# Second half's high parts parked in DRAM, low parts left in place; one gate tile in a third buffer

## Chip, cores and metric

One Trainium2 chip, one of its cores. The metric is the device time of one execution in microseconds, the median of the runs shown. Every time below is in microseconds unless it says ns.

## What is computed

The input `x` holds 32 sequences of 64 rows with 1024 values. A state-space convolution (a kernel of length 1024 for each of the 64 channels, masked by each sequence's length) makes a matrix of 2048 rows (tokens) by 1024. A feed-forward block with 4-bit packed weights follows, and its result is added to `x`:

```
x2    = conv(x).reshape(2048, 1024)
w[k,n] = q[k,n]*s[k//128, n] - (z[k//128, n] + 1)*s[k//128, n]
gate  = x2 @ Wg            # 1024 x 2752
up    = x2 @ Wu            # 1024 x 2752
inter = gate * sigmoid(gate) * up
out   = x + (inter @ Wd).astype(float16)    # Wd: 2752 x 1024
```

## The kernel before, in words

The convolution comes first and leaves its result in SBUF. The second half of the rows (1024 tokens) stays as plain float32 in `y2` until it is needed. The matrix products take their operands in the reduced 32-bit form, so that every moving operand is split into a high part (a cast) and a low part (value minus high part), and each product is made twice, once with each.

The feed-forward block then runs in tiles `tau` = 0 to 43: 22 tiles of 128 intermediate columns for the first 1024 rows, and the same 22 for the second 1024 (`NT` = 22 is the first tile of the second half). The last tile of each half (`TAIL` = 21, and `LAST` = 43) is narrow: 64 gate columns and 64 up columns share one gate tile, so it has no up products, and its down products are half as many.

A tile has eight slots `g`, one for each group of 128 input features. In a slot TensorE does `gate(tau, g)` (four matmuls, L1186), `down` of one 128-column piece of an earlier tile (four matmuls, L1225; it lags by 11 slots) and `up(tau, g)` (four matmuls, L1207). ScalarE rescales the gate and up sums between groups (L631, L650). VectorE takes each down piece into `acc` (`take_down`, L951), unpacks weights (`shift`, L889, then `center`, L913; gate in slots 1 and 2, up in 3 and 4, down in 5 and 6), and multiplies gate by up once a tile (`multiply`, L929). GpSimd splits that product into `mid_h` and `mid_l` (`split_mid`, L517 and L520). The down pieces use two PSUM pairs in turn, so `down` number n waits for `take_down` number n-2.

The order of work on every engine is written out by hand, and so is that of the DMA queue: SyncE issues the weight loads in `LOAD_ORDER` into a ring of four buffers `q_in`, each load waiting until the one four places before it has been centered.

At the border of the halves the operand `xs` is replaced. In tile 21 ScalarE casts `y2` into the high parts of `xs` as soon as the gate products of a group have used the old ones (L660), and GpSimd makes the low parts (`split_x2`, L527), four before `split_mid(21)` and four behind it. `gate(22, g)` waits for them. The narrow tile's down weights are shifted and centered together in slot 7 of tile 21.

At the end, `down_last` (L1243) does the 16 half-width pieces of tile 43, of which GpSimd sums seven (`BY_POOL`, L555, from what ScalarE has scaled, L670) and VectorE nine (L975). The output of 1024 rows is stored in eight pieces of 512 KB: in six of them TensorE adds `x` and the turned result in PSUM (`rows_first`, L1255, `rows_second`, L1266) and ScalarE copies the sum out (L677); in two VectorE adds (L984). Before `down_last` VectorE splits the narrow product (`split_last`, L965).

Of the kernel before, what the change touches and what calls it, by code (L numbers as in the profile page):

```python
# [16 lines left out]
P = 128  # L17
# [3 lines left out]
KT = L // P  # L21
# [20 lines left out]
TURN_AT, TURN_STEP = 181, 8  # L42
TINY = float(2.0 ** -60)
# [85 lines left out]
def load_order():  # L129
    order = [("g", 0), ("u", 0), ("d", 0), ("g", 1), ("u", 1)]  # L130
    for tau in range(1, TILES):
        order += [("g", tau + 1)] * (tau + 1 < TILES)
        order += [("u", up_after(tau))] * (up_after(tau) is not None)
        order += [("d", tau)]
    return order

# [5 lines left out]
BY_POOL = (0, 3, 5, 7, 9, 11, 13)  # L142
THROUGH_PE = (0, 1, 2, 3, 6, 7)
# [15 lines left out]
def build_program(nc, x, itok, log_dt, C, log_A, A_imag, D, gq, gs, gz, uq, us, uz, dq, ds, dz,  # L159
                  ctab, stab, ident_in, out):  # L160
    kpad = nc.dram_tensor("kernel_padded", (H, KPAD), F32, kind="Internal").ap()
    rows_back = nc.dram_tensor("rows_backwards", (2 * TAIL + 1, 16, G, P), I32, kind="Internal").ap()
    zscr = nc.dram_tensor("zeros_plus_one", (3, ROWS, P), BF16, kind="Internal").ap()
    with ExitStack() as ctx:
# [9 lines left out]
        xs = sb("xs", [P, 2, KT, HALF], F32R)  # L174
# [55 lines left out]
        o16 = sb("o16", [P, NH, HALF], F16)  # L230
        x_fin = sb("x_fin", [P, 4, HID])
# [11 lines left out]
        w["d"][1] = sb("wd1", [P, HID], F32R)  # L243

# [30 lines left out]
        x2_cast, x2_split = sem("x2_cast"), sem("x2_split")  # L275
# [10 lines left out]

        def up_ps(tau):

            return pair[3] if tau else pair[1]

        def last_ps(e):

            return (pair[3], pair[0])[e // 2 % 2][:, e % 2, :]

        def last_turn_ps(tt):
            return pair[3][:, tt % 2, :].bitcast(F16)
# [22 lines left out]
        def _(sp):  # L319
# [138 lines left out]
            for tau in range(1, TILES):  # L458
                if tau + 1 < TILES:
# [26 lines left out]
            for tt in range(HALF_G):  # L486
                if tt in THROUGH_PE:
                    sp.wait_ge(sum_copied, 2 * (THROUGH_PE.index(tt) + 1))
# [7 lines left out]
        def _(pool):  # L496
# [7 lines left out]
            for g in range(HALF_G):  # L504
                pool.wait_ge(x1_cast, g + 1)
                here = slice(P * g, P * g + P)
                pool.tensor_tensor(xs[:, 1, :, here], y_nat[:, g % 2], xs[:, 0, :, here].bitcast(F32), ALU.subtract  # L507
# [16 lines left out]
            def split_x2(kt):  # L524

                pool.wait_ge(x2_cast, kt + 1)
                pool.tensor_tensor(xs[:, 1, kt, :], y2[:, kt, :], xs[:, 0, kt, :].bitcast(F32), ALU.subtract  # L527
                                   ).then_inc(x2_split, 1)

            def cast_out(hid):  # L530

                pool.wait_ge(x2_split, KT)
# [830 lines left out]
```

## Time and profile before

| what | value |
|---|---|
| median of 3 runs | 1199.46 (1198.85 to 1199.54) |
| profiled execution: own time | 1200.26 |
| profiled execution: span of its records | 1198.2 |
| mean granted TensorE clock | 0.992 |
| TensorE matmul busy | 97% |
| VectorE, ScalarE, GpSimd busy | 75%, 72%, 18% |

The span runs from the first to the last record of the core. Busy shares are averages over the whole span; a stage can have another limit than the whole.

### The profile page before, as it was taken

The numbers are of one execution on the slowest core, as the hardware profiler recorded it, in microseconds if no ns is written. First come the engines' busy times: TensorE is split into PE (matmuls) and PEld (weight loads), VectorE is DVE, ScalarE is ACT, GpSimd is POOL, SyncE is SP. The second block draws the span as 40 slices with busy tenths as digits, with TensorE's granted clock in tenths as the row PEclk, the third lists the DMA queues.
The fourth block names the chain that finished last, engine by engine and source line by source line (L and its number), as shares of the span: only waits on it lengthen the run. The fifth ranks groups of instructions, "written<-read, shape, count | busy, mean of one in ns | idle before, by whom it ended". The sixth has DMA issues, their size and how long they took to land.

```text
span 1198.2 us, 15016 instructions
## 1 busy us (share of the span) xinstructions
PE 1164.7 (97%) x5570; PEld 953.6 (80%) x5570; DVE 896.6 (75%) x964; ACT 859.7 (72%) x1408; POOL 213.3 (18%) x126
## 2 busy tenths in 40 slices
PE   5899999999999999999999899999999999999997
PEld 4899999788788788788788678888788788788784
DVE  7698755677777777777777888887777777777775
ACT  6433213888788788788788877778788788788774
POOL 0022000211211211211211851211211211211212
PEclk9899999999999999999999999999999999999999
DMA  8587868434444334444444355555434443444413
GB/s 294 171 263 245 274 222 247 129 99 112 106 102 110 106 103 108 106 106 106 106 106 106 79 176 147 170 169 147 106 100 112 106 104 108 106 105 107 150 59 152
DMA packets 64670, 165.54 MB, mean 138 GB/s; under 512 B 11398, under 2 KB 16966, under 8 KB 64598
## 3 DMA queue, kind: packets, MB, share of 16 engines
q1 hardware_dynamic: 64566, 164.56, 47.8%
q8 instruction: 44, 0.72, 0.3%
q14 instruction: 28, 0.23, 0.1%
q0 software_dynamic: 32, 0.03, 0.0%
HBM read 155.74 MB, written 11.64 MB: 140 GB/s over the span
## 4 chain that ended last, share of the span: by engine, by line
PE 86%; DVE 4%; SPq 3%; issue 2%; DMA 2%; ACT 1%; POOL 0%; ACTq 0%; DVEq 0%; POOLq 0%
PE pair L1186 26%; PE pair L1207 26%; PE pair L1225 25%; PE pair L1143 8%; DMA toep<-kernel_padded 1%; DVE acc L951 1%; SPq L333 1%; ACT pair L631 1%; PE pair L1255 1%; DVE q_in L889 1%; DMA kernel_padded<-k_sb 1%; ACT xs L660 1%; POOL o L555 0%; DVE arg L712 0%; DVE y_nat L847 0%
## 5 line engine op out<-in xcount | busy, mean ns | idle before, releaser
L951 DVE SCALAR_TENSOR_TENSOR acc<-pair,s_down,acc 128x1024 f32<-128x1024 f32 x328 | 420.6, 1283 | 209.1 <-PE pair L1225 209.0
L650 ACT ACTIVATE pair<-pair,ratio 128x512 f32<-128x512 f32 x581 | 360.6, 658 | 130.7 <-PE pair L1207 130.7
L631 ACT ACTIVATE pair<-pair,ratio 128x512 f32<-128x512 f32 x616 | 382.6, 666 | 97.1 <-PE pair L1186 96.7
L1186 PE MATMUL pair<-xs,wg 128*128 128x512 f32 x1408 | 388.7, 398 | 0.1
L1207 PE MATMUL pair<-xs,wu 128*128 128x512 f32 x1344 | 368.7, 395 | 1.9 <-DVE sil L929 1.9
L1186 PEld LDWEIGHTS pair<-xs,wg 128*128 128x128 f32 x1408 | 264.8, 189 | 64.6 <-ACT pair L631 4.1
L1207 PEld LDWEIGHTS pair<-xs,wu 128*128 128x128 f32 x1344 | 249.4, 188 | 67.2 <-issue 11.7
L1225 PE MATMUL pair<-mid_h,wd 128*128 128x512 f32 x688 | 268.6, 392 | 5.4 <-DVE acc L951 5.4
L1225 PE MATMUL pair<-mid_l,wd 128*128 128x512 f32 x672 | 265.8, 396 | 0.0
L517 POOL CAST mid_h<-sil 128x1024 fp32r<-128x1024 f32 (+1 forms) x43 | 45.2, 1051 | 843.2 <-DVE sil L929 841.8
L1225 PEld LDWEIGHTS pair<-mid_h,wd 128*128 128x128 f32 x688 | 129.4, 188 | 37.9 <-DVE acc L951 6.9
L1143 PE MATMUL pair<-u_all,toep 128*128 128x256 f32 (+7 forms) x1024 | 151.9, 310 | 5.2 <-DMA toep<-kernel_padded 5.2
L1143 PEld LDWEIGHTS pair<-u_all,toep 128*128 128x128 f32 x1024 | 147.0, 193 | 9.6 <-DMA toep<-kernel_padded 5.7
L1225 PEld LDWEIGHTS pair<-mid_l,wd 128*128 128x128 f32 x672 | 126.2, 188 | 30.4
L520 POOL TENSOR_TENSOR mid_l<-sil,mid_h 128x1024 fp32r<-128x1024 f32 x42 | 101.8, 2424 | 3.4
L889 DVE TENSOR_SCALAR q_in<-q_in,shifts 128x1024 int32<-128x1024 int32 x130 | 101.8, 783 | 0.0
L642 ACT ACTIVATE sil<-pair,ratio 128x512 f32<-128x512 f32 (+1 forms) x88 | 55.8, 693 | 0.7 <-PE pair L1186 0.7
L913 DVE TENSOR_TENSOR wg<-q_in,z_in 128x1024 fp32r<-128x1024 int32 x44 | 56.1, 1276 | 0.1
L913 DVE TENSOR_TENSOR wd<-q_in,z_in 128x1024 fp32r<-128x1024 int32 x44 | 55.4, 1260 | 0.1
L929 DVE SCALAR_TENSOR_TENSOR sil<-pair,ratio,sil 128x1024 f32<-128x1024 f32 x42 | 53.6, 1275 | 1.2 <-PE pair L1207 1.2
L913 DVE TENSOR_TENSOR wu<-q_in,z_in 128x1024 fp32r<-128x1024 int32 x42 | 51.0, 1215 | 0.0
L507 POOL TENSOR_TENSOR xs<-y_nat,xs 128x1024 fp32r<-128x1024 f32 x8 | 20.0, 2503 | 103.4 <-ACT xs L620 103.4
(156 smaller groups left out, 424.2 us busy)
## 6 DMA issues: line engine op xcount, KB each, us to landing
q_in<-rows_backwards SPq DMA_DIRECT2D x86, 512.0 KB, 4.6
z_in<-zeros_plus_one SPq DMA_DIRECT2D x130, 256.0 KB, 4.6
toep<-kernel_padded SPq DMA_DIRECT2D x64, 512.0 KB, 6.7
q_in<-_L_ffn_down_qweight_dram SPq DMA_DIRECT2D x42, 512.0 KB, 4.6
u_all<-in_x_dram SPq DMA_DIRECT2D x16, 512.0 KB, 9.1
x_fin<-in_x_dram SPq DMA_DIRECT2D x12, 512.0 KB, 8.4
out_dram<-x_fin SPq DMA_DIRECT2D x12, 512.0 KB, 5.3
q_in<-in_x_dram SPq DMA_DIRECT2D x4, 512.0 KB, 5.5
```

The costliest lines, as they stand in the source:

```text
L520: pool.tensor_tensor(low, whole, mid_h[0:n, tau % 2].bitcast(F32), ALU.subtract).then_inc(midl_done, 1)
L631: act.activation(gate_ps[:, tb, :], gate_ps[:, tb, :], ACT.Copy, scale=ratio[:, 0, G * t + g:G * t + g + 1]).then_inc(gate_scaled, 1)
L642: act.activation(sil[to:to + n, tb, :], gate_ps[0:n, tb, :], ACT.Silu, scale=ratio[0:n, 0, G * t + G - 1:G * t + G]).then_inc(gate_scaled, 1)
L650: act.activation(up_ps(tau)[:, tb, :], up_ps(tau)[:, tb, :], ACT.Copy, scale=ratio[:, 1, G * t + g:G * t + g + 1]).then_inc(up_scaled, 1)
L889: dve.tensor_scalar(q_in[slot][:], q_in[slot][:], shifts[:, m == "d":1 + (m == "d")], 15, ALU.logical_shift_right, ALU.bitwise_and).then_i ...
L913: dve.tensor_tensor(to, q, z, ALU.subtract).then_inc(centered, 1)
L929: dve.scalar_tensor_tensor(out=sil[:], in0=up_ps(tau)[:], scalar=ratio[:, 1, G * t + G - 1:G * t + G], in1=sil[:], op0=ALU.mult, op1=ALU.m ...
L951: dve.scalar_tensor_tensor(out=acc[:, hid, :], in0=ps, scalar=scale, in1=acc[:, hid, :], op0=ALU.mult, op1=ALU.add).then_inc(down_taken, 1)
L1143: mm = pe.matmul(conv_ps[half_][k][:, base + B * d:base + 256], toep[:, slot, P * (KT - 1 - d):P * (KT - d)], u_all[:, g, 0:KT - d, B * hh ...
L1186: mm = pe.matmul(gate_ps[:, tb, :], w["g"][tau % 2][:, g, :], xs[:, part, g, 512 * tb:512 * tb + 512], start=g == 0 and part == 0, stop=pa ...
L1207: mm = pe.matmul(up_ps(tau)[:, tb, :], w["u"][full_before(tau) % 2][:, g, :], xs[:, part, g, 512 * tb:512 * tb + 512], start=g == 0 and pa ...
L1225: mm = pe.matmul(down_ps[at % 2][:, tb, :], w["d"][tau % 2][:, P * hid:P * hid + P], mid[:, tau % 2, 512 * tb:512 * tb + 512], start=part ...
```

## The change

- The split of the second half moves from tiles 21 and 22 to tiles 4 to 11, all of it on GpSimd (`split_second`): in tile 4+kt, once that tile's down weights are centered, it casts `y2[:, kt]` into `staged` (512 KB) and subtracts that from `y2` in place, which makes `low_2`. SyncE stores `staged` in a DRAM tensor `high_parts`, behind the load of that tile's down weights, and GpSimd waits for the store before it uses `staged` again.
- At the border SyncE loads the eight high parts (512 KB each) into `high`, each after `gate(21, kt)`; ahead of them stand the loads of gate and up 23, behind them those of down 22 and of four pieces of `x`.
- The gate tile 22 is loaded behind up 22 and shifted and centered in slot 4 of tile 20, into a third buffer. The narrow tile's down weights are shifted in slot 5 of tile 21 and centered in slot 0 of tile 22.
- At the end the last two pieces of tile 42 go to the PSUM pairs of up and gate, `down_last` to the down pairs, the split of the narrow product moves to GpSimd, `BY_POOL` becomes (0, 1, 4, 6, 8, 11, 13), four output pieces go through TensorE and four through VectorE, and the stores go in the order 0, 1, 4, 5, 2, 6, 3, 7.
- `low_1` (first half) lies where `o16` and `x_fin` come later.

```diff
@@ load_order
-        order += [("g", tau + 1)] * (tau + 1 < TILES)
+        order += [("g", tau + 1)] * (tau + 1 < TILES and tau != TAIL)
         order += [("u", up_after(tau))] * (up_after(tau) is not None)
+        order += [("g", NT)] * (tau == TAIL - 1)
         order += [("d", tau)]
...
-BY_POOL = (0, 3, 5, 7, 9, 11, 13)
-THROUGH_PE = (0, 1, 2, 3, 6, 7)
+BY_POOL = (0, 1, 4, 6, 8, 11, 13)
@@ sync
+                if tau == TAIL - 1:
+                    load_weights("g", NT)
+                if tau == NT:
+                    sp.wait_ge(high_stored, 16 * KT)
+                    for kt in range(KT):
+                        sp.wait_ge(gate_mm, 2 * (G * TAIL + kt) + 2)
+                        sp.dma_start(high[:, kt, :].bitcast(F32), high_back[kt]).then_inc(high_in[kt], 16)
                 load_weights("d", tau)
-                if tau == NT + 1:
-                    sp.wait_ge(x2_split, KT)
+                if SPLIT_FROM <= tau < SPLIT_FROM + KT:
+                    sp.wait_ge(high_staged, tau - SPLIT_FROM + 1)
+                    sp.dma_start(high_back[tau - SPLIT_FROM], staged[:].bitcast(F32)).then_inc(high_stored, 16)
+                if tau == NT:
                     for tt in range(4):
                         load_x(0, tt)
@@ gpsimd
+            def split_second(kt):
+                if kt:
+                    pool.wait_ge(high_stored, 16 * kt)
+                else:
+                    pool.wait_ge(y_ready, 2 * NG)
+                pool.wait_ge(centered, load_at("d", SPLIT_FROM + kt) + 1)
+                pool.tensor_copy(staged[:], y2[:, kt, :]).then_inc(high_staged, 1)
+                pool.wait_ge(high_staged, kt + 1)
+                pool.tensor_tensor(low_2[:, kt, :], y2[:, kt, :], staged[:].bitcast(F32), ALU.subtract
+                                   ).then_inc(low_ready, 1)
...
             for tau in range(LAST):
-                if tau == TAIL:
-                    for kt in range(4):
-                        split_x2(kt)
+                if SPLIT_FROM <= tau < SPLIT_FROM + KT:
+                    split_second(tau - SPLIT_FROM)
                 split_mid(tau)
                 if tau == TAIL:
-                    for kt in range(4, KT):
-                        split_x2(kt)
@@ scalar
-                    if tau == TAIL:
-                        act.copy(xs[:, 0, g, :], y2[:, g, :]).then_inc(x2_cast, 1)
@@ vector
-                    if g == G - 1 and tau == TAIL:
+                    if g == 5 and tau == TAIL:
                         shift("d", TAIL)
+                    if g == 0 and tau == NT:
                         center("d", TAIL)
...
                         if g == 4:
                             center("u", up_after(tau))
+                            if tau == TAIL - 1:
+                                shift("g", NT)
+                                center("g", NT)
@@ tensor
+                if tau == NT and g == 0:
+                    pe.wait_ge(low_ready, KT)
                 if tau == NT:
-                    pe.wait_ge(x2_split, g + 1)
+                    pe.wait_ge(high_in[g], 16)
...
+                if tau == LAST - 1 and hid == NH - 1:
+                    pe.wait_ge(last_mid, 2)
+                elif at >= 2 and not (tau == LAST - 1 and hid == NH - 2):
                     pe.wait_ge(down_taken, at - 1)
...
-            down(LAST - 1, NH - 3)
-            down(LAST - 1, NH - 2)
+            for hid in range(NH - 3, NH):
+                down(LAST - 1, hid)
             for e in range(4):
                 down_last(e)
-            down(LAST - 1, NH - 1)
             rows_first(0)
             down_last(4)
             down_last(5)
             rows_first(1)
-            for e in range(6, 12):
+            for e in range(6, 11):
                 down_last(e)
             rows_second(0)
-            down_last(12)
-            down_last(13)
             rows_second(1)
-            down_last(14)
-            down_last(15)
+            for e in range(11, 16):
+                down_last(e)
             rows_first(2)
+            turn_last(4)
+            turn_last(5)
             rows_second(2)
             rows_first(3)
+            turn_last(6)
             rows_second(3)
-            turn_last(4)
-            turn_last(5)
-            rows_first(6)
-            rows_second(6)
-            rows_first(7)
-            rows_second(7)
+            turn_last(7)
```

## Rows read from the trace of the kernel before

**Rows 1.** The page: busy time, share of the span, instructions, by engine.

```profile
PE 1164.7 (97%) x5570; PEld 953.6 (80%) x5570; DVE 896.6 (75%) x964; ACT 859.7 (72%) x1408; POOL 213.3 (18%) x126
```

**Rows 2.** TensorE's timeline at the border: start, duration, operation, count, idle before.

```profile
658.98 1.10 PE L1186 MATMUL pair<-xs,wg 128*128 128x512 f32 x4
...
676.23 1.20 PE L1186 MATMUL pair<-xs,wg 128*128 128x512 f32 x4
...
685.34 0.50 PE L1225 MATMUL pair<-mid_h,wd 128*128 128x512 f32 x1 [3.26 <-DVE acc L951]
...
703.48 1.55 PE L1207 MATMUL pair<-xs,wu 128*128 128x512 f32 x4 [1.93 <-DVE sil L929]
...
710.68 1.10 PE L1186 MATMUL pair<-xs,wg 128*128 128x512 f32 x4
```

**Rows 3.** Busy time by stretch: last columns are granted clock, DMA share, GB/s.

```profile
705.00:707.40 2.40, 2.40 (x8) 1.83 (x7) 0.00 (x0) 1.95 (x3) 2.40 (x2) 0.50 1.08 413
```

**Rows 4.** VectorE's timeline at the border.

```profile
680.87 3.21 DVE L913 TENSOR_TENSOR wd<-q_in,z_in 128x1024 fp32r<-128x1024 int32 x1
684.01 2.46 DVE L951 SCALAR_TENSOR_TENSOR acc<-pair,s_down,acc 128x1024 f32<-128x1024 f32 x2
```

**Rows 5.** GpSimd's timeline at the border.

```profile
680.30 11.20 POOL L527 TENSOR_TENSOR xs<-y,xs 128x1024 fp32r<-128x1024 f32 x4
```

**Rows 6.** Line 660, ScalarE's casts: ns min, median, max; first and last start.

```profile
L660 ACT CAST xs<-y x8: 1047/1088/1137, 660.8 to 675.8; 128x1024 fp32r<-128x1024 f32 x8
```

**Rows 7.** GpSimd's timeline in tiles 5 and 6.

```profile
302.40 1.04 POOL L517 CAST mid_h<-sil 128x1024 fp32r<-128x1024 f32 x1 [18.88 <-DVE sil L929]
...
324.80 1.04 POOL L517 CAST mid_h<-sil 128x1024 fp32r<-128x1024 f32 x1 [18.88 <-DVE sil L929]
325.92 2.40 POOL L520 TENSOR_TENSOR mid_l<-sil,mid_h 128x1024 fp32r<-128x1024 f32 x1
```

**Rows 8.** VectorE's timeline in tiles 5 and 6.

```profile
329.14 0.74 DVE L889 TENSOR_SCALAR q_in<-q_in,shifts 128x1024 int32<-128x1024 int32 x1
330.73 1.28 DVE L951 SCALAR_TENSOR_TENSOR acc<-pair,s_down,acc 128x1024 f32<-128x1024 f32 x1 [0.84 <-PE pair L1225]
```

**Rows 9.** TensorE's timeline in tile 6.

```profile
335.17 0.39 PE L1225 MATMUL pair<-mid_h,wd 128*128 128x512 f32 x1
```

**Rows 10.** The DMA queue's timeline between tiles 5 and 6.

```profile
321.92 0.53 SPq L417 DMA_DIRECT2D q_in<-rows_backwards  x1
```

**Rows 11.** The page's DMA issues: count, size, median from issue to landing.

```profile
z_in<-zeros_plus_one SPq DMA_DIRECT2D x130, 256.0 KB, 4.6
```

**Rows 12.** Line 447, loads of `x`, from 698 to 703.

```profile
DMA to landing us min/median/max: 6.6/7.8/10.1
```

**Rows 13.** TensorE's timeline at the end.

```profile
1166.46 1.08 PE L1186 MATMUL pair<-xs,wg 128*128 128x512 f32 x4
...
1172.68 1.21 PE L1243 MATMUL pair<-mid_h,wd 128*128 128x512 f32 x4 [0.71 <-DVE mid_h L965]
...
1181.75 0.61 PE L1266 MATMUL pair<-ident,o 128*128 128x128 f16 x8 [0.88 <-POOL o L555]
...
1191.19 1.94 PE L1255 MATMUL pair<-q_in,ident 128*128 128x512 f32 x4
```

**Rows 14.** ScalarE's timeline at the end.

```profile
1193.61 1.07 ACT L677 COPY q_in<-pair 128x512 f32<-128x512 f32 x2 [1.15 <-PE pair L1266]
```

**Rows 15.** GpSimd's timeline at the end.

```profile
1180.33 5.08 POOL L555 TENSOR_TENSOR o<-z_in,acc 128x512 f16<-128x512 f32 x4 [0.91 <-ACT z_in L670]
```

**Rows 16.** VectorE's timeline at the end.

```profile
1169.43 2.48 DVE L951 SCALAR_TENSOR_TENSOR acc<-pair,s_down,acc 128x1024 f32<-128x1024 f32 x2
```

**Rows 17.** Line 451, stores from 1160 on: their issues, then issue to landing.

```profile
L451 SPq DMA_DIRECT2D out_dram<-q_in x4: 538/538/586, 1190.0 to 1194.7; - x4
...
DMA to landing us min/median/max: 3.0/3.0/3.7
```

**Rows 18.** Busy time by stretch, as rows 3.

```profile
1192.00:1194.00 2.00, 1.57 (x11) 0.72 (x9) 0.00 (x0) 0.85 (x2) 0.00 (x0) 1.00 1.01 414
```

More of the change, by code:

```diff
@@ L274, in build_program @@
         down_mm, down_taken = sem("down_mm"), sem("down_taken")
-        x2_cast, x2_split = sem("x2_cast"), sem("x2_split")
+        high_staged, high_stored, low_ready = sem("high_staged"), sem("high_stored"), sem("low_ready")
+        high_in = [sem(f"high_in{i}") for i in range(KT)]
         o16_done = sem("o16_done")
@@ L285, in build_program, with parts_of @@
         gate_ps, down_ps = pair[0], [pair[1], pair[2]]
+        def parts_of(tau):
+            return high, (low_2 if tau >= NT else low_1)
         def up_ps(tau):
@@ L458, in _ @@
             for tau in range(1, TILES):
-                if tau + 1 < TILES:
+                if tau + 1 < TILES and tau != TAIL:
                     load_weights("g", tau + 1)
@@ L688, in _ @@
                     copy_sum(1)
-            for tt in THROUGH_PE[2:]:
+            for tt in (2, 3):
                 copy_sum(tt)
@@ L1058, in _ @@
                         continue
-                    if tau + 1 < TILES:
+                    if tau + 1 < TILES and tau != TAIL:
                         if g == 1:
@@ L1087, in _ @@
                     take_last(e)
-            for tt in (4, 5):
+            for tt in range(4, HALF_G):
                 finish_last(tt)
@@ L1184, in gate @@
                         pe.wait_ge(gate_scaled, 2 * (G * tau + g) - 1 + tb)
-                    for part in range(2):
-                        mm = pe.matmul(gate_ps[:, tb, :], w["g"][tau % 2][:, g, :],
-                                       xs[:, part, g, 512 * tb:512 * tb + 512],
+                    for part, rows in enumerate(parts_of(tau)):
+                        mm = pe.matmul(gate_ps[:, tb, :], w["g"][gate_slot(tau)][:, g, :],
+                                       rows[:, g, 512 * tb:512 * tb + 512],
                                        start=g == 0 and part == 0, stop=part == 1, skip_group_check=g > 0)
@@ L1205, in up @@
                         pe.wait_ge(first_up_scaled, g)
-                    for part in range(2):
+                    for part, rows in enumerate(parts_of(tau)):
                         mm = pe.matmul(up_ps(tau)[:, tb, :], w["u"][full_before(tau) % 2][:, g, :],
-                                       xs[:, part, g, 512 * tb:512 * tb + 512],
+                                       rows[:, g, 512 * tb:512 * tb + 512],
                                        start=g == 0 and part == 0, stop=part == 1, skip_group_check=g > 0)
```

92 lines of the change are left out of this document (49 added, 43 removed).

## The prediction

> **What bounds the kernel now.** The page comes first: TensorE is busy for 97% of the span [rows 1], no other engine over 75%. So a saving must take matmul time away (the change takes none) or close the holes in TensorE's own timeline. That timeline is read next. In a steady tile it has none: `split_mid` starts every 22.40 us [rows 7], that is 2.80 a slot, or 0.93 for each of the slot's three blocks of four matmuls. The holes are at the border of the halves and at the end, and the reader is to look at those two stretches only.
>
> At the border, `gate(21, 0)` starts at 658.98 and `gate(23, 3)` at 710.68: 51.70 us [rows 2]. Between them TensorE waits 3.26 us for `take_down` and 1.93 us for `multiply` [rows 2]. VectorE's timeline says why it is late: a `center` that takes 1.22 elsewhere took 3.21 [rows 4] while GpSimd made four low parts without a pause, 680.30 to 691.5 [rows 5]. The takes beside it, which read PSUM, kept their 1.23 each [rows 4]. So the holes come from VectorE's weight unpacking standing behind GpSimd. After the second hole the granted clock was 0.50 (1.2 GHz) in 705.00 to 707.40 [rows 3], and that costs as well.
>
> **Term 1: the border.** I count what TensorE has to do there, with nothing late. Tile 21: eight slots of gate and down, 8 x 1.86 = 14.88, and the `down` ahead of `gate(22, 0)` 0.93: 15.8. The trace took 17.25 (676.23 less 658.98) [rows 2], since ScalarE had a cast of 1.09 in each slot beside its two scalings [rows 6]; the casts are gone. Does the gate bank come free in time? The first half of the last gate product, ScalarE's half of it (about 0.7) and VectorE's (about 0.7) need some 2.1 us after `gate(21, 7)` starts, and TensorE has gate, down, down, 2.8 us, of its own. Yes. Tile 22: slot 0 has no second down (1.86), slots 1 and 2 are full (5.60), from slot 3 on `down` is the narrow one, half of 0.93, so 2.33 a slot: five of them 11.65; then three such slots of tile 23, 7.0. Sum 15.8 + 19.1 + 7.0 = 41.9.
>
> What can be late in it: VectorE. With slot 0 of tile 22 at T, it has two takes to T+2.5, then the `center` of down 21, which stands behind `split_mid(21)` until about T+3.6 and ends at T+4.8. The narrow `down` needs it at T+8.4. From there a shift or center with a take (2.0 and 2.5) goes against slots of 2.33, and `multiply(22)` ends at about T+20.8, where `up(23, 0)` could start at T+20.5. I charge 0.35 for it. So 42.2 against 51.7: **-9.5 us**. Bounds: nothing charged, -9.8; if ScalarE's five operations of about 2.5 a slot and the late take are both felt, some 2 us more, -7.5.
>
> The high parts must be there. Load kt starts after `gate(21, kt)`, the last of them 14 us after the first. Loads of 512 KB packed together landed 6.6 to 10.1 us after issue [rows 12], and each is first read 15 us or more after its issue: hidden. Behind them on the queue stand down 22 (needed at T+14.9) and four pieces of `x`; both have over 5 us. Gate 23 and up 23 are ahead of them, and their buffers are free in tile 20. Tile 20, slot 4 gets a shift and a center more, 0.74 + 1.22. It is hidden by the take's slack: `take_down` of slot 2 ends at 332.0 in tile 6 [rows 8] and the `down` that needs its bank starts at 335.17 [rows 9], 3.2 us later. Without that cover it would cost the 1.96.
>
> **Term 2: tiles 4 to 11.** GpSimd gets a cast and a subtraction, 1.04 + 2.40 by [rows 7], after `center` of the down weights. In the clock of tiles 5 and 6 that center ends at 321.9 (there the queue issues the load that waited for it [rows 10]), so GpSimd is at work to 325.5, and `split_mid`, which started at 324.80, comes 0.8 later and ends at 329.1. Its reader, `down` in slot 3, starts at about 332.4. Hidden.
>
> The wait that is added stands on SyncE. The store waits for `high_staged`, and behind it stands the load of gate tau+2. Before, it was issued at 321.92 [rows 10] for a shift 29.6 us later (329.14 [rows 8] plus a tile). Now it is issued a tile later, at 321.9 + 1.1 (cast) + 0.6 (store's issue) = 323.6, for the shift at 329.14: 5.5 us ahead. A weight load's second part lands 4.6 after its own issue [rows 11], 0.57 later: 328.8 if the store took no bandwidth. At 414 GB/s [rows 18] the store's 512 KB hold the queue 1.27: 330.1. Upper bound of the likely: a load of `x` right behind one weight load landed 6.6 after its issue [rows 12], so 324.2 + 6.6 = 330.8. VectorE's shift is late by 1.0 (bounds 0 and 1.7). Behind it on VectorE stands the take of slot 2, which had 0.84 of idle before it [rows 8] and may itself be late by 3.2 [rows 8, 9] before TensorE stands: 4.0. So **0**, with a margin of 2.3 or more a tile, for eight tiles. Without it each us late would cost eight.
>
> The Trainium skill speaks on the same transfer: "DMA: Bandwidth & Descriptors", section "Anatomy of one DMA", gives a fixed 2.0 us and the bytes at 436 GB/s. As an estimate, store and load (1.31 MB) land 5.0 us after the store's issue, at 328.0, ahead of the shift, where the rows say 330.1; the sum is the same by both.
>
> **Term 3: the end.** All in the clock of before. `gate(43, 7)` starts at 1166.46 [rows 13]; gate and four downs now follow without a hole, to 1171.1. `down_last(0)` needs the take that ends at 1170.7 [rows 16] and GpSimd's split of 64 x 512 (1.27, as its sums [rows 15]), about 1170.9. It starts at 1171.1 instead of 1172.68 [rows 13]. GpSimd has the 4th sum of `BY_POOL` as the one that `rows_second(0)` waits for: piece 6 is multiplied at 1176.9, scaled to 1177.6, summed to 1178.9. So `rows_second(0)` is at 1179.0 instead of 1181.75 [rows 13]. Then copies of 1.07 [rows 14], two fp32 `rows_first` of 1.77, which start at 1182.0 and 1185.3, and adds of about 1.2 give the eight pieces at 1182.0, 1183.7, 1185.7, 1186.9, 1187.5, 1188.8, 1189.4 and 1190.0, the last instead of 1194.7 [rows 17]: 4.7 earlier. But stores are now packed: one alone lands in 3.0, packed ones in 3.7 [rows 17], a step of 1.27 each at 414 GB/s [rows 18] (524 KB). From 1185.7 + 3.0 five more steps give 1195.0, where before it was 1194.7 + 3.0 = 1197.7. So **-2.7 us**. Bounds: unpacked -4.7; if a hand-over in the new order stands 2 us longer, -0.7.
>
> Sum: -9.5 + 0 - 2.7 = -12.2. Profiled span 1198.2 to 1186.0, its own time 1200.26 to 1188.1. The median lies 0.8 below the profiled execution; on it, 1199.46 - 12.2 = **1187.3**.
>
> **The rivals.** (A) Forecast, chance 0.76: own range 1185 to 1190.
>
> (B) The late gate load becomes TensorE's wait in tiles 5 to 12. It decides once the landing is more than 4.0 us behind the shift's place, at 333.1, 8.9 us after the second part's issue. For it: the loads among `x` took up to 10.1 [rows 12], and the store shares the queue. Against it: those had 2 MB ahead, this one has 0.8. At 10.1 the stall is 1.2 a tile, eight tiles 9.6: 1196.9. A milder one, 0.5 a tile, gives 1191.3. Chance 0.10 together, of it 0.03 for the other side: from 1.5 a tile on, twelve and more, the kernel is not faster; at 2 a tile and a half-speed clock behind each hole (some 1 us) it is 24 - 12.2, 1211.
>
> (C) The end gives nothing, as its stores are bound by the DMA engines or the new hand-over waits: -9.5 alone, 1190.0. Chance 0.08.
>
> (D) The border stays half open, because VectorE, not GpSimd, is the limit: the casts' 1.4 us and the first hole go, the second hole and its slow clock (about 3.5) stay: -6 - 2.7, 1190.8. For it: VectorE has 2.0 or 2.5 of work in slots of 2.33. Against it: it was late there by the 3.2 and 2.8 us operations. Chance 0.05. The rest, 0.01, is that the time doesn't change.
>
> One rule would bring (D) or (B) forward. The Trainium skill, "SBUF — State Buffer", section on the two sides of ports: VectorE operations with two SBUF inputs and GpSimd operations lock each other out for a whole instruction, whoever starts first. The trace agrees at the border (3.21 against 1.22). By it a center that starts first could hold GpSimd's split up by 1.2 a tile, still hidden.
>
> **Range and chances.** Eight times in ten: 1185.0 to 1191.5, which takes in (C), (D) and the mild (B). A change of 0.2%, 2.4 us, is what a measurement tells from none. Faster: A, C, D and most of B, 0.95. Same: 0.02. Slower: 0.03.
>
> **What would show it.** Right: no wait over 0.5 between 655 and 700 on TensorE, granted clock 1.00 there, `gate(23, 3)` 42 us after `gate(21, 0)`; tiles 5 to 12 at 22.40, with VectorE's gate shift about 1 us late on a DMA; `rows_second(0)` 2.7 earlier against `gate(43, 7)`; stores of 3.7 and more. Wrong: tiles 5 to 12 over 22.6, with `acc` as TensorE's releaser; a hole before `up(23, 0)` of over 1 us.

## The result and the profile after

The changed kernel takes **1186.56 us** (median, 1184.68 to 1190.44), the kernel before beside it on the same chip 1199.5 (1198.85 to 1201.85). The ratio is 0.9893, with an interval of 0.9863 to 0.9923: 1.1% faster. Predicted were 1187.3.

The profiled execution of after took 1190.44 by its own time, with a span of 1188.7 and a mean granted clock of 0.991. It stands 3.9 above its median, where that of before stood 0.8 above. The reason lies ahead of everything that the change touches: its first tile starts 4.0 later (below). So I read the change from stretches between two marks, not from the two spans.

The page of after, busy time by engine, answers to [rows 1]:

```profile
PE 1158.5 (97%) x5562; PEld 955.3 (80%) x5562; DVE 891.3 (75%) x964; ACT 848.7 (71%) x1396; POOL 220.8 (19%) x136
```

ScalarE has lost its eight casts and GpSimd gained work; TensorE is still the bound. TensorE's timeline of after gives the marks. In order: `gate(21, 0)`, `gate(22, 0)`, the one hole left ahead of `up(23, 0)`, `gate(23, 3)`, `gate(43, 7)`, `down_last(0)`, `rows_second(0)`. It answers to [rows 2, 13].

```profile
662.95 0.39 PE L1224 MATMUL pair<-high,wg 128*128 128x512 f32 x1
...
678.72 0.39 PE L1224 MATMUL pair<-high,wg 128*128 128x512 f32 x1
...
699.48 0.47 PE L1245 MATMUL pair<-high,wu 128*128 128x512 f32 x1 [0.40 <-DVE sil L973]
...
705.08 0.39 PE L1224 MATMUL pair<-high,wg 128*128 128x512 f32 x1
...
1157.93 0.40 PE L1224 MATMUL pair<-high,wg 128*128 128x512 f32 x1
...
1162.51 0.62 PE L1283 MATMUL pair<-mid_h,wd 128*128 128x512 f32 x2
...
1171.24 1.05 PE L1305 MATMUL pair<-ident,o 128*128 128x128 f16 x16 [0.94 <-POOL o L600]
```

Subtract neighbours in both profiles and the span falls into four stretches:

| stretch | before | after | difference | predicted |
|---|---|---|---|---|
| start to `gate(21, 0)` | 658.98 | 662.95 | +4.0 | 0 |
| to `gate(23, 3)`: the border | 51.70 | 42.13 | -9.57 | -9.5 |
| to `gate(43, 7)`: second half | 455.78 | 452.85 | -2.93 | 0 |
| to the end of the span | 31.74 | 30.77 | -0.97 | -2.7 |

The first row isn't the change. The first tile's product on VectorE starts at 213.51 before and at 217.52 after, and from there to the product of tile 20 both take the same (445.95 and 445.99): the 4.0 arise in the convolution, which the change leaves as it is. Over the 14 profiles of this case, whose convolution is the same, that mark lies anywhere from 211.98 to 218.05: the border and the end alone, parts of the same change, have 211.98 and 212.78. In this profile the granted clock falls to 0.91 in one stretch of it, where before and the border alone have 1.00 and the short low parts (first tile at 218.05) 0.91 as well (TensorE, first and last columns but two; the last three are granted clock, DMA share and GB/s):

```profile
180.00:200.00 20.00, 18.21 (x118) 17.67 (x116) 7.88 (x8) 0.00 (x0) 0.00 (x0) 0.91 1.04 336
```

**The border.** The granted clock behind the last hole, where [rows 3] had 0.50:

```profile
698.00:700.00 2.00, 1.60 (x7) 1.05 (x6) 2.00 (x3) 1.24 (x2) 0.60 (x1) 1.00 1.05 239
```

VectorE's timeline of after shows the `center` of down 21 and the next shift, which answer to [rows 4]. The shift took 0.73; the one behind [rows 4] took 2.83 (started at 686.40), as long as GpSimd made low parts:

```profile
681.31 2.24 DVE L957 TENSOR_TENSOR wd<-q_in,z_in 128x1024 fp32r<-128x1024 int32 x1
684.66 0.73 DVE L932 TENSOR_SCALAR q_in<-q_in,shifts 128x1024 int32<-128x1024 int32 x1
```

and GpSimd's timeline what stood beside the `center`: `split_mid(21)`'s subtraction. Before had that one too, at 677.82; the 11.20 of [rows 5], the low parts, are gone:

```profile
680.07 2.40 POOL L555 TENSOR_TENSOR mid_h<-sil,mid_h 64x1024 fp32r<-64x1024 f32 x1
```

**Tiles 4 to 11.** VectorE in tile 6: the take, then the gate shift, which now waits for a transfer. It answers to [rows 8]:

```profile
331.91 1.28 DVE L995 SCALAR_TENSOR_TENSOR acc<-pair,s_down,acc 128x1024 f32<-128x1024 f32 x1 [1.61 <-PE pair L1265]
...
334.08 0.75 DVE L932 TENSOR_SCALAR q_in<-q_in,shifts 128x1024 int32<-128x1024 int32 x1 [0.89 <-DMA z_in<-zeros_plus_one]
```

The waits of the whole run, this one in total, count and longest:

```profile
DVE q_in L932 <- DMA z_in<-zeros_plus_one: 6.1, 8, 1.9
```

It occurs eight times, once a tile, as the change has it, and TensorE shows nothing of it: tiles 4 to 11 take 22.40 each, as before. GpSimd in tile 6 (cast and low part of the second half, then `split_mid`) and the queue between tiles 5 and 6 (store, then the load behind it) answer to [rows 7, 10]:

```profile
325.99 1.04 POOL L566 CAST staged<-y 128x1024 fp32r<-128x1024 f32 x1 [15.40 <-DVE wd L957]
327.11 2.40 POOL L568 TENSOR_TENSOR low<-y,staged 128x1024 fp32r<-128x1024 f32 x1
329.46 1.03 POOL L552 CAST mid_h<-sil 128x1024 fp32r<-128x1024 f32 x1
```

```profile
327.06 0.32 SPq L499 DMA_DIRECT2D high_parts<-staged  x1
327.42 0.53 SPq L443 DMA_DIRECT2D q_in<-rows_backwards  x1
```

**The second half.** VectorE's product of gate and up starts once a tile, so its distance is the tile's period. Three in a row:

```profile
900.51 1.28 DVE L973 SCALAR_TENSOR_TENSOR sil<-pair,ratio,sil 128x1024 f32<-128x1024 f32 x1
...
922.82 1.28 DVE L973 SCALAR_TENSOR_TENSOR sil<-pair,ratio,sil 128x1024 f32<-128x1024 f32 x1
...
944.98 1.27 DVE L973 SCALAR_TENSOR_TENSOR sil<-pair,ratio,sil 128x1024 f32<-128x1024 f32 x1
```

22.31 and 22.16, and 22.25 on the mean of the tiles from 28 on, where before had 22.40 in both halves and after still has it in its first. No hole of TensorE was closed there, since there was none. That is the part that the prediction had not seen.

**The end.** ScalarE, GpSimd, VectorE's last two adds, and the queue's last stores, which answer to [rows 15, 17]:

```profile
1169.06 1.27 ACT L713 ACTIVATE z_in<-pair,s_down 128x512 f32<-128x512 f32 x2 [1.49 <-PE pair L1283]
```

```profile
1169.83 2.50 POOL L600 TENSOR_TENSOR o<-z_in,acc 128x512 f16<-128x512 f32 x2 [0.92 <-ACT z_in L713]
```

```profile
1180.11 2.36 DVE L1020 TENSOR_TENSOR q_in<-pair,q_in 128x1024 f32<-128x1024 f16 x2 [0.76 <-PE pair L1314]
```

```profile
1178.25 2.09 SPq L477 DMA_DIRECT2D out_dram<-q_in  x2
1181.95 1.12 SPq L477 DMA_DIRECT2D out_dram<-x_fin  x1
1183.12 1.18 SPq L477 DMA_DIRECT2D out_dram<-q_in  x1
```

```profile
DMA to landing us min/median/max: 3.8/4.4/5.2
```

The last fence is the stores' time from issue to landing from 1175 on; it was 3.0, 3.0 and 3.7 [rows 17].

### The profile page after: what moved, and what is told of

The parts are those of the page before. It is cut to its first block, busy times and chain, and to the rows that moved or that the text cites. A ratio compares the mean times of both kernels' runs of the same rounds, so it can differ in the third digit from the quotient of the medians.

```text
span 1188.7 us, 15014 instructions
## 1 busy us (share of the span) xinstructions
PE 1158.5 (97%) x5562; PEld 955.3 (80%) x5562; DVE 891.3 (75%) x964; ACT 848.7 (71%) x1396; POOL 220.8 (19%) x136
## 4 chain that ended last, share of the span: by engine, by line
PE 94%; SPq 3%; DMA 1%; issue 1%; POOL 0%; DVE 0%; ACT 0%; DVEq 0%; POOLq 0%
PE pair L1224 27%; PE pair L1245 26%; PE pair L1265 26%; PE pair L1179 12%; DMA toep<-kernel_padded 1%; SPq L359 1%; DMA kernel_padded<-k_sb 0%; PE pair L1159 0%; POOL o L600 0%; PE pair L1294 0%; PE pair L1327 0%; SPq L384 0%; PE pair L1139 0%; SPq L386 0%; SPq L395 0%
## 5 line engine op out<-in xcount | busy, mean ns | idle before, releaser
L1224 PE MATMUL pair<-high,wg 128*128 128x512 f32 x704 | 278.6, 396 | 0.0
L1224 PE MATMUL pair<-low,wg 128*128 128x512 f32 x704 | 276.9, 393 | 0.0
L1245 PE MATMUL pair<-high,wu 128*128 128x512 f32 x672 | 267.6, 398 | 0.4 <-DVE sil L973 0.4
L1245 PE MATMUL pair<-low,wu 128*128 128x512 f32 x672 | 263.4, 392 | 0.0
L1179 PE MATMUL pair<-u_all,toep 128*128 128x256 f32 (+7 forms) x1024 | 155.4, 315 | 5.5 <-DMA toep<-kernel_padded 5.5
L1224 PEld LDWEIGHTS pair<-high,wg 128*128 128x128 f32 x704 | 132.1, 188 | 31.5 <-ACT pair L676 1.1
L1245 PEld LDWEIGHTS pair<-high,wu 128*128 128x128 f32 x672 | 126.1, 188 | 38.5 <-issue 10.5
L1224 PEld LDWEIGHTS pair<-low,wg 128*128 128x128 f32 x704 | 132.8, 189 | 29.5
L1245 PEld LDWEIGHTS pair<-low,wu 128*128 128x128 f32 x672 | 126.3, 188 | 27.3
L932 DVE TENSOR_SCALAR q_in<-q_in,shifts 128x1024 int32<-128x1024 int32 x130 | 97.8, 753 | 6.1 <-DMA z_in<-zeros_plus_one 6.1
```

What stands on the lines that cost most here:

```text
L932: dve.tensor_scalar(q_in[slot][:], q_in[slot][:], shifts[:, m == "d":1 + (m == "d")], 15, ALU.logical_shift_right, ALU.bitwise_and).then_i ...
L1179: mm = pe.matmul(conv_ps[half_][k][:, base + B * d:base + 256], toep[:, slot, P * (KT - 1 - d):P * (KT - d)], u_all[:, g, 0:KT - d, B * hh ...
L1224: mm = pe.matmul(gate_ps[:, tb, :], w["g"][gate_slot(tau)][:, g, :], rows[:, g, 512 * tb:512 * tb + 512], start=g == 0 and part == 0, stop ...
L1245: mm = pe.matmul(up_ps(tau)[:, tb, :], w["u"][full_before(tau) % 2][:, g, :], rows[:, g, 512 * tb:512 * tb + 512], start=g == 0 and part = ...
```

## The experiments

Each profile is read by the same marks, from VectorE's timeline: m0 is the start of the first tile's product, m20 that of tile 20, and so on; "end" is from the product of tile 43 to the span's end. Between m42 and the product of tile 43 lie 14.0 more, 13.8 in "small tables between", and 13.7 in the five kernels whose tiles take 21.97; the table leaves them out. Worked out from the starts:

| kernel | m0 | m0 to m20 | m20 to m22 | m22 to m42 | end | median |
|---|---|---|---|---|---|---|
| before | 213.51 | 445.95 | 42.60 | 451.89 | 30.23 | 1199.5 |
| after | 217.52 | 445.99 | 34.54 | 447.38 | 29.26 | 1186.6 |
| border alone | 211.98 | 446.16 | 34.55 | 448.36 | 30.14 | 1188.5 |
| end alone | 212.78 | 446.03 | 42.56 | 450.63 | 29.28 | 1198.1 |
| two more stores | 215.43 | 451.46 | 34.55 | 447.25 | 29.20 | 1193.8 |
| four more stores | 212.53 | 484.30 | 34.54 | 447.06 | 28.56 | 1222.8 |
| short low parts | 218.05 | 445.97 | 37.95 | 451.22 | 30.19 | 1199.5 |
| small tables between | 214.50 | 442.88 | 34.19 | 446.69 | 29.22 | 1183.1 |
| small tables behind | 212.27 | 437.84 | 33.84 | 441.75 | 29.19 | 1170.4 |
| small tables first | 215.88 | 437.61 | 33.80 | 441.73 | 29.17 | 1173.7 |
| behind, 512 bytes on | 213.08 | 437.67 | 33.80 | 442.25 | 29.19 | 1171.6 |
| behind, 128 bytes on | 213.85 | 446.13 | 34.75 | 450.57 | 29.27 | 1190.4 |
| before, placed anew | 212.11 | 437.37 | 42.50 | 441.56 | 30.24 | 1181.9 |
| behind, piece 13 moved | 213.55 | 437.63 | 33.86 | 441.56 | 28.88 | 1172.7 |

Kernels with one execution have that one in the last column: both with more stores, the short low parts, and those with 512 and 128 bytes. The column m22 to m42 holds the last piece of the border too, and repeats to about 1: 447.38 and 448.36 for the same text up to the end, 451.89 and 450.63 in before and the end alone.

### The change in two parts

**The border alone.** After, with the end of before:

```diff
-BY_POOL = (0, 1, 4, 6, 8, 11, 13)
+BY_POOL = (0, 3, 5, 7, 9, 11, 13)
+THROUGH_PE = (0, 1, 2, 3, 6, 7)
...
-            pool.wait_ge(down_mm, down_at(LAST - 2, NH - 1) + 1)
-            for tb in range(2):
...
+            def split_last(tb):
```

> The change with the end of before (order of the last pieces, split by VectorE, stores 0 to 7). Theory: border and end add. The stretch from gate(21,0) to gate(23,3) is the changed kernel's, 42.1 us against 51.7, and from gate(43,7) to the end of the span it is before's 31.7 us. The second half's tiles are also below 22.40 us, as in the changed kernel (22.16 and 22.31), since that does not hang on the end. Rival: the faster tiles come from the new end's use of the PSUM pairs or not from this part, and are gone here. Time: about 1.0 us above the changed kernel, near 1187.5.

Measured: 1188.51 (1187.0 to 1192.1), ratio 0.9914 (0.989 to 0.9938). The border is 34.55, as in after; the end 30.14, as in before; the second half is quick here too (448.36).

**The end alone.** Before, with the new end, the same hunk the other way round.

> The kernel before with the new end alone. Theory: 0.9 to 1.0 us less from gate(43,7) to the end of the span (30.8 against 31.7), nothing elsewhere, tiles of 22.40 in both halves: near 1198.5. Rival, the prediction's own term: 2.7 us less, 1196.8.

Measured: 1198.07 (1196.26 to 1201.06), ratio 0.9988 (0.9976 to 1.0001). In the profile the end is 29.28 instead of 30.23, and the second half keeps its 22.41 a tile. The two parts add up: the end is worth about 0.9 whichever border stands ahead of it. The prediction's -2.7 falls; its rival that the end gives nothing was nearer, though the profiles show more than nothing. The median can't tell 0.9 from none.

This profile shows one thing more. Its border is that of before, GpSimd's low parts included, and `gate(21, 0)` to `gate(23, 3)` took 50.10 (658.33 to 708.43), where before took 51.70. The first hole is the same (3.27), the second shrank to 0.42:

```profile
702.78 1.17 PE L1211 MATMUL pair<-xs,wu 128*128 128x512 f32 x4 [0.42 <-DVE sil L945]
```

The granted clock tells why. Behind the first hole it was 0.50 here, and 1.00 in before (the two rows in this order):

```profile
684.33:688.33 4.00, 3.64 (x9) 2.88 (x10) 4.00 (x3) 0.66 (x1) 4.00 (x3) 0.50 0.72 197
```

```profile
684.98:688.98 4.00, 3.65 (x16) 2.99 (x17) 4.00 (x3) 1.96 (x4) 4.00 (x3) 1.00 0.77 197
```

From product 20 to product 22 both took the same, 42.56 and 42.60. So the slow stretch came while VectorE was behind anyway, and TensorE only arrived later at a wait that it had in any case. In before the slow stretch came behind the second hole [rows 3], where nothing covers it. The same text costs 1.6 more or less by that.

### Is GpSimd what holds VectorE up at the border?

Before, with the low parts of the second half made of 8 columns instead of 1024, so that GpSimd is hardly busy, and the order of work as it was (the other 1016 columns of those low parts are left out):

```diff
-                pool.tensor_tensor(xs[:, 1, kt, :], y2[:, kt, :], xs[:, 0, kt, :].bitcast(F32), ALU.subtract
+                pool.tensor_tensor(xs[:, 1, kt, 0:8], y2[:, kt, 0:8], xs[:, 0, kt, 0:8].bitcast(F32), ALU.subtract
```

> The kernel before, in which GpSimd makes the eight low parts at the border for 8 of 1024 columns only (the rest of the second half's low parts is left out); the casts and everything else stay. Theory (VectorE is late because GpSimd holds it up): the two holes of 3.26 and 1.93 and the slow clock behind them go; gate(21,0) to gate(23,3) falls from 51.7 to 43 or 44, the 1.4 of ScalarE's casts being left. Rival (VectorE has too much to do in slots of 2.33): the second hole stays, 47 or more.

TensorE's timeline of this kernel:

```profile
663.54 1.10 PE L1186 MATMUL pair<-xs,wg 128*128 128x512 f32 x4
...
687.90 0.49 PE L1225 MATMUL pair<-mid_h,wd 128*128 128x512 f32 x1 [1.25 <-DVE acc L951]
...
703.39 1.18 PE L1207 MATMUL pair<-xs,wu 128*128 128x512 f32 x4 [0.33 <-DVE sil L929]
...
709.04 1.10 PE L1186 MATMUL pair<-xs,wg 128*128 128x512 f32 x4
```

`gate(21, 0)` to `gate(23, 3)` is 709.04 - 663.54 = 45.50, against 51.70 in before and 50.10 in the end alone: 4.6 to 6.2 go with GpSimd's work and nothing else. From product 20 to product 22, where the place of the slow clock doesn't matter, it is 37.95 against 42.60 and 42.56. The holes went from 3.26 and 1.93 to 1.25 and 0.33, and the drop of the clock is gone. That is a little more left than I expected. The rest has its reasons in the profile: ScalarE's casts (some 1.5), and the 1.25, where shift and center of the narrow tile's weights still follow each other and the shift stands behind `split_mid(21)` (0.74 elsewhere, here 2.88):

```profile
682.44 2.88 DVE L889 TENSOR_SCALAR q_in<-q_in,shifts 128x1024 int32<-128x1024 int32 x1
```

So the rival by which VectorE alone keeps the border half open falls: with its work unchanged, and TensorE at a granted clock of 1.00 from the first hole to the second as in before, the second hole shrank from 1.93 to 0.33. The clock has to be named here, since the end alone shows a second hole of 0.42 for another reason. The whole time, 1199.48, shows no gain because this execution's first tile started 4.5 later than before's (218.05); the border's gain is inside it.

### How far is the late load from costing something?

After, with the store of `staged` made three times, twice into a tensor that nobody reads, then five times:

```diff
                     sp.dma_start(high_back[tau - SPLIT_FROM], staged[:].bitcast(F32)).then_inc(high_stored, 16)
+                    for again in range(2):
+                        sp.dma_start(unread[again, tau - SPLIT_FROM], staged[:].bitcast(F32)).then_inc(high_stored, 16)
```

> The changed kernel with each of its eight stores made three times (two of them to a DRAM tensor that nobody reads), ahead of the loads. The margin of 4.0 us that the prediction gave the late gate shift, tested: in the changed kernel the shift waits 0.5 to 1.9 us for its landing; two stores of 1.27 us more make that 3.0 to 4.4. Theory: still hidden, tiles 5 to 12 stay at 22.40 (one perhaps 0.4 over). Rival: the margin is smaller or the clock drops, and the tiles grow by 1 us or more each.

> The same with each store made five times: the shift is late by 5.6 to 6.9 us. Theory: past the margin of 4.0, so that tiles 5 to 12 take 1.6 to 2.9 us more each, 13 to 23 us in all, TensorE waiting for take_down (acc). Rival, that SyncE's queue hides it or that the stores overlap: less than 5 us in all.

With two more, VectorE's shift and TensorE's next `down` in tile 6:

```profile
336.52 0.75 DVE L935 TENSOR_SCALAR q_in<-q_in,shifts 128x1024 int32<-128x1024 int32 x1 [4.45 <-DMA z_in<-zeros_plus_one]
```

```profile
338.52 0.50 PE L1268 MATMUL pair<-mid_h,wd 128*128 128x512 f32 x1 [0.34 <-DVE acc L998]
```

The eight shifts together, by the waits from 290 to 500:

```profile
DVE q_in L935 <- DMA z_in<-zeros_plus_one: 36.2, 8, 5.0
```

36.2 / 8 = 4.5 late, and the eight tiles take 5.5 more than 8 x 22.40, 0.7 each (0.2 to 1.2). I had expected them still hidden, with one at most 0.4 over; they weren't. TensorE begins to stand at 4.5 - 0.7, about 3.8: near the margin of 4.0 that the prediction worked out from [rows 8, 9]. In after the shift waits 0.45 to 1.89. One thing was off: I had a store at 1.27; two cost (36.2 - 6.1) / 8 = 3.8, 1.9 each. Part of it is SyncE itself: the two issues behind the stores took 1.15 and 1.16 instead of 0.53 and 0.62.

With four more, the same two instructions, and the window behind the hole:

```profile
339.46 0.75 DVE L935 TENSOR_SCALAR q_in<-q_in,shifts 128x1024 int32<-128x1024 int32 x1 [6.94 <-DMA z_in<-zeros_plus_one]
```

```profile
341.46 0.50 PE L1268 MATMUL pair<-mid_h,wd 128*128 128x512 f32 x1 [2.83 <-DVE acc L998]
```

```profile
340.00:345.00 5.00, 3.54 (x9) 2.79 (x10) 5.00 (x6) 0.81 (x2) 0.00 (x0) 0.70 0.81 186
```

The eight holes are 2.1 to 3.5, 24.1 together, and the eight tiles take 38.3 more, 4.8 each. The other 1.8 a tile go with the clock: granted 0.70 in that window, so part of it ran at 1.2 GHz, and 0.30 of 5 us is 1.5. I had expected 13 to 23 in all, without a term for the clock. It is the price at which the prediction's rival with the late load would have ended on the slower side: 1222.78.

### Where do 2.9 us of the second half come from?

First theory: the two passes of a block read operands that lie nearer each other (or farther apart) than in before, and distance sets the pace. Rival: it is the place of the operand against the weights. In after six small tables (`ratio`, `s_down`, `shifts`, `ident16`, `ident`, `warm`; 2,944 bytes a partition together) lie behind `x_fin`. I moved them, and nothing else, to between `high` and `low_1`, then behind the last weight buffer:

```diff
         high = sb("high", [P, KT, HALF], F32R)
-        with ExitStack() as half_1:
-            low_1 = half_1.enter_context(nc.sbuf_tensor("low_1", [P, KT, HALF], F32R))
-        o16 = sb("o16", [P, NH, HALF], F16)
-        x_fin = sb("x_fin", [P, 4, HID])
         ratio = sb("ratio", [P, 2, ROWS])
...
         warm = sb("warm", [P, 1])
+        with ExitStack() as half_1:
+            low_1 = half_1.enter_context(nc.sbuf_tensor("low_1", [P, KT, HALF], F32R))
+        o16 = sb("o16", [P, NH, HALF], F16)
+        x_fin = sb("x_fin", [P, 4, HID])
```

```diff
         x_fin = sb("x_fin", [P, 4, HID])
-        ratio = sb("ratio", [P, 2, ROWS])
...
-        warm = sb("warm", [P, 1])
...
         w["g"].append(sb("wg2", [P, G, P], F32R))
+        ratio = sb("ratio", [P, 2, ROWS])
...
+        warm = sb("warm", [P, 1])
```

> The changed kernel with the small tables (2.9 KB a partition) placed between high and low_1, so that high and low parts of the first half no longer stand exactly 32 KB apart; all else is the same program. Theory A (the place of the low parts to the high parts sets the pace of the matmuls that read them): the tiles of the first half fall from 22.40 to the 22.16 to 22.31 of the second, some 2 to 4 us over 21 tiles. Theory B (the second half's pace has another cause, such as the values, the clock or how the low parts were made): the first half stays at 22.40.

> The changed kernel with the small tables placed behind all tensors, so that low_2 stands exactly 64 KB from high. Theory A (distance): the second half's tiles go back to 22.40, some 2 to 3 us more; the first half stays at 22.40. Theory B: nothing changes, 22.16 to 22.31 in the second half.

Two products in a row in the first half, between:

```profile
434.85 1.28 DVE L973 SCALAR_TENSOR_TENSOR sil<-pair,ratio,sil 128x1024 f32<-128x1024 f32 x1
...
457.16 1.28 DVE L973 SCALAR_TENSOR_TENSOR sil<-pair,ratio,sil 128x1024 f32<-128x1024 f32 x1
```

and behind:

```profile
408.08 1.27 DVE L973 SCALAR_TENSOR_TENSOR sil<-pair,ratio,sil 128x1024 f32<-128x1024 f32 x1
...
430.06 1.27 DVE L973 SCALAR_TENSOR_TENSOR sil<-pair,ratio,sil 128x1024 f32<-128x1024 f32 x1
```

22.31 between, in turn with 22.16 (22.24 on the mean), so that this first half now has the second half's pace, and 21.98 behind, in both halves. My theory of the distance had the second of them at 22.40: it fell. The medians are 1183.06 (0.9863, 0.984 to 0.9886) and 1170.42 (0.9765, 0.9744 to 0.9786). The second is faster than the changed kernel by another 16.

What fits the order of all of them is the offset of a matmul's moving operand against its weights, taken modulo 512 bytes; 2,944 is 5.75 x 512. In before, `xs` is at a multiple of 4 KB, and the weights and `mid` lie 2,944 on: 8 of a slot's 12 matmuls are off. In after's second half `low_2` is at +2,944 as the weights are and `high` isn't: 4 of 12. With the tables behind, none. Three kernels asked that theory: the tables ahead of everything (all at +2,944 alike), and, with them behind, a pad of 512 bytes (below) and of 128 bytes (`[P, 32]`) between the operands and the weights:

```diff
         low_2 = sb("low_2", [P, KT, HALF], F32R)
+        sb("pad", [P, 128])
         acc = sb("acc", [P, NH, HALF])
```

> The changed kernel with the small tables (2,944 bytes a partition) ahead of all tensors: high, both low parts, mid and the weights then all stand 2,944 bytes off the multiples of 4 KB, with the same distances between them as in e4, where all stand on such multiples. Theory D (the pace of a matmul hangs on how its moving operand and its weights stand to each other): tiles near 21.97 in both halves, near 1171 in all. Theory C (what counts is that each tensor starts on a round address): tiles of 22.2 or more.

> e4 with 512 bytes left free ahead of acc, so that mid and the weights move by 512 against high and low. Theory D with a modulus of 512 or less: 21.97 stays. Theory D with a larger modulus, or theory C with round addresses above 512: over 22.1.

> e4 with 128 bytes left free ahead of acc. Theory D with a modulus of 512 (a group of weights is 512 bytes a partition) and theory C alike: tiles of 22.3 or 22.4. With a modulus of 128 or less: 21.97.

512 bytes:

```profile
408.85 1.27 DVE L974 SCALAR_TENSOR_TENSOR sil<-pair,ratio,sil 128x1024 f32<-128x1024 f32 x1
...
430.81 1.28 DVE L974 SCALAR_TENSOR_TENSOR sil<-pair,ratio,sil 128x1024 f32<-128x1024 f32 x1
```

128 bytes:

```profile
413.42 1.27 DVE L974 SCALAR_TENSOR_TENSOR sil<-pair,ratio,sil 128x1024 f32<-128x1024 f32 x1
...
435.83 1.27 DVE L974 SCALAR_TENSOR_TENSOR sil<-pair,ratio,sil 128x1024 f32<-128x1024 f32 x1
```

21.96 and 22.41, and 21.95 with the tables first (1173.73, 0.9774, 0.9747 to 0.9802). A shift by 512 bytes costs nothing, one by 128 bytes the whole 0.43 a tile. If each matmul that is off cost the same, 4 of 12 would make 22.18 a tile. After has 22.25 on the mean of its second half and "between" 22.24 and 22.21 in its two, so the count gives the order but not the size.

Two things stay open. TensorE's starts show that the time isn't lost in the matmuls that are off alone. The `down` block, whose operand `mid` and weights have equal offsets in every one of these kernels, took 0.93 in before:

```profile
921.99 0.39 PE L1225 MATMUL pair<-mid_h,wd 128*128 128x512 f32 x1
...
922.92 1.09 PE L1207 MATMUL pair<-xs,wu 128*128 128x512 f32 x4
```

and 0.91 in "before, placed anew", the kernel below:

```profile
922.69 0.39 PE L1226 MATMUL pair<-mid_h,wd 128*128 128x512 f32 x1
...
923.60 1.07 PE L1208 MATMUL pair<-xs,wu 128*128 128x512 f32 x4
```

And in all these runs the weights, `mid`, `sil` and `acc` moved together against `high` and the low parts. So what is shown is that the pace hangs on where the operands lie against the buffers behind them, modulo 512 bytes; that the weights are the ones that count was not tested apart.

Last, the same edit on the kernel before, with neither its border nor its end touched (a pad of 8 KB keeps the tables clear of what later takes that room):

```diff
         xs = sb("xs", [P, 2, KT, HALF], F32R)
-        ratio = sb("ratio", [P, 2, ROWS])
...
-        warm = sb("warm", [P, 1])
...
         w["d"][1] = sb("wd1", [P, HID], F32R)
+        sb("pad", [P, 2048])
+        ratio = sb("ratio", [P, 2, ROWS])
...
+        warm = sb("warm", [P, 1])
```

> The kernel before, with the small tables behind all tensors (and 8 KB free ahead of them, since the convolution's buffers reach there), so that its operands stand on multiples of 4 KB. Theory: the placement acts alone, tiles of 21.97 instead of 22.40 in both halves, some 17 to 18 us less than before, near 1182; the border keeps its holes, so e4 stays 12 us below it. Rival: the pace belongs to the changed kernel (its in-place low parts), and the tiles here stay at 22.40.

Two products of its first half:

```profile
407.86 1.28 DVE L930 SCALAR_TENSOR_TENSOR sil<-pair,ratio,sil 128x1024 f32<-128x1024 f32 x1
...
429.82 1.28 DVE L930 SCALAR_TENSOR_TENSOR sil<-pair,ratio,sil 128x1024 f32<-128x1024 f32 x1
```

Measured: 21.96 a tile, 1181.88 (1179.53 to 1185.85), 0.9847 (0.982 to 0.9874): placement alone gives about 18, more than the whole change. From here to "behind", 1181.9 to 1170.4, is 11.5: the border's and the end's gain stays when the pace is the same in both.

### One more hand-over at the end

GpSimd makes seven of the last sums; with the tables behind I gave one of them, piece 13, to VectorE:

```diff
-BY_POOL = (0, 1, 4, 6, 8, 11, 13)
+BY_POOL = (0, 1, 4, 6, 8, 11)
...
-                if e == 13:
-                    copy_sum(1)
-            for tt in (2, 3):
+            for tt in (1, 2, 3):
```

> e4 (operands on round addresses) with piece 13 of the last tile summed by VectorE instead of GpSimd, so that ScalarE copies the second output piece at once. Theory: the hand-over of GpSimd's last sum is what the end waits for, and it comes 0.5 to 0.7 us earlier: near 1170 against e4's 1170.4, and 0.3 to 0.7 less from the last gate product to the end. Rival: the end is bound by its eight packed stores, and nothing is gained.

TensorE's `rows_second(0)` still waits for GpSimd as long as in after:

```profile
1152.12 1.05 PE L1303 MATMUL pair<-ident,o 128*128 128x128 f16 x16 [0.94 <-POOL o L600]
```

Measured: the end is 28.88 instead of 29.19, 0.3 less, and the medians, 1172.65 (1171.02 to 1173.59) and 1170.42 (1169.33 to 1173.1) on another chip, can't be told apart. Inconclusive as a gain. The fastest version remains the changed kernel with its small tables behind the weights: 1170.42, 0.9765 of before.

## Why the prediction was right, and where its sum was not

**Border, right.** Predicted -9.5, measured -9.57, and the steps hold one by one: `gate(21, 0)` to `gate(22, 0)` 15.77 (15.8 predicted), one hole of 0.40 ahead of `up(23, 0)` (0.35), clock 1.00. That it agrees to 0.1 is partly luck: 51.70 is one execution of before, and the same border took 50.10 in another, by which the gain is 8.0. The cause was tested on its own: GpSimd's idleness alone gave 4.6 to 6.2. The Trainium skill, "SBUF — State Buffer", section "SBUF: two separate sides", says that a two-input VectorE operation and a GpSimd operation exclude each other. By that rule, the trace agrees: `center` took 2.24 beside `split_mid(21)`, and there it had slack to spare. The shift, with one tensor input, was held up as well: 2.88 for 0.74 beside GpSimd in the kernel with short low parts.

**Tiles 4 to 11, right.** Nothing lost. The shift was predicted 1.0 late in tile 6 and was 0.89 late (0.45 to 1.89 over the eight), and the margin of 4.0 was found at about 3.8. The rival with the late load had its mechanism and its threshold right; with two stores more than there are it costs 0.7 a tile.

The price of one store was too low: 1.27 by the bandwidth, 1.9 by the runs. It didn't matter at one store a tile. From the store's issue to the late shift the rows gave 7.1 (323.0 to 330.1), and after took 7.0 (327.06 to 334.08). The 5.0 that the prediction estimated by the Trainium skill, "DMA: Bandwidth & Descriptors", was short; its section "Anatomy of one DMA" describes DMAs issued by GpSimd, and these are SyncE's.

**End, mis-sized.** The step that failed is "So **-2.7 us**": it measured -0.97, inside its bounds (-4.7 and -0.7). In the clock of before (8.53 added, by `gate(43, 7)`), `down_last(0)` was at 1171.0, as predicted (1171.1). `rows_second(0)` came at 1179.8 instead of 1179.0, since ScalarE, which waited 1.49 for TensorE's piece 6, scaled it from 1177.6 instead of 1176.9. The first adding store was issued at 1186.8 instead of 1185.7, and the last at 1191.65 instead of 1190.0: packed issues take SyncE 1.12 and 1.18 each, where [rows 17] had 0.54, and I had priced only their bytes. It landed 5.2 later (5.0 predicted). So of the missing 1.7, 0.8 is the hand-over through ScalarE and GpSimd, the rest the step from one add and store to the next. Of that rest the issues are the larger part: VectorE's last add ended at 1182.47, and its store was issued at 1183.12, when SyncE had done with the issue at 1181.95. That is 0.65, read from the profile, not tested.

**Not predicted: the second half, -2.93.** The sum had no term for where the operands lie, although the diff moved them (`high`, `low_1`, `low_2` for `xs`). The experiments show it: it comes with the border's edit and its new buffers ("border alone" has it, "end alone" has not), and it moves with the tables.

**The total.** -9.57 - 2.93 - 0.97 is -13.5 in the profiles, with the convolution's 4.0 taken out, and the medians differ by 12.9; predicted were -12.2. The time fell in the likeliest case, 0.7 from the forecast, and that nearness is luck: the end's 1.7 too much and the pace's 2.9 too little partly cancelled. Without that pace the measured border and end give -10.5 together, some 1189, which is in the range too.

## What to carry to other kernels

A hole in the bound engine's timeline behind an operation that takes twice its usual time is worth the whole hole and the slow clock behind it: look for which other engine was busy at that moment, and move that engine's work to where the bound engine has slack, even at the price of a round trip through DRAM. When a slow clock follows, look whether the bound engine had a wait ahead of it anyway: with the slow stretch behind the last hole instead of the first, the same border was 1.6 us longer. Work out the slack of a new wait as a number (here 4.0 against 1.0) before counting it as hidden. And when buffers move, compare the steady pace of a tile before and after: 2,944 bytes of small tables between the operands and the buffers behind them cost 18 us here, where nothing in the profile showed a wait, and 512 bytes cost nothing.

## What was not expected of the hardware

- The pace of these matmuls hangs on the moving operand's address against that of the buffers behind it, the weights among them: 21.97 a tile with equal offsets modulo 512 bytes, 22.40 with 8 of 12 matmuls off by 128 or 384 bytes (2,944 modulo 512), no idle time in either. All three blocks of a slot are longer, `down` too (0.93 for 0.91). An offset of 256 wasn't run, and why it is so stays open.
- Stores packed on one queue cost more than their bytes: 1.9 each where the bandwidth gives 1.27, with issues behind them of 1.15 instead of 0.53.
- Holes of 2.1 to 3.5 on TensorE made tiles 4.8 longer each: the granted clock was 0.70 in the 5 us around the one of 2.83, while with holes of 0.2 to 0.9 it stayed at 1.00. But the drop doesn't follow every long hole at once: behind the same hole at the border, 3.26 and 3.27, it was 1.00 in before and 0.50 in the end alone.
- The convolution's length differs by 6 us between profiles of kernels that share its text (first tile at 211.98 to 218.05), with a granted clock of 0.91 in 180 to 200 of the one shown.
